# Converting the next batch block's edge-mask pieces on GpSimd at the head of each attention unit, instead of on VectorE between the row maxima

## The chip, the cores and the metric

The kernel runs on one core of a Trainium2 chip. The metric is the device time of one execution in microseconds (us), as the median of several runs. Engines are called PE (TensorE), DVE (VectorE), ACT (ScalarE), POOL (GpSimd) and SP (the sync engine, which here only issues DMAs).

## What is computed

A graph-attention layer over 2048 nodes of width 256 with a dense 2048 by 2048 edge mask, and after it a mixture of 8 experts, of which every token takes two. The part that matters here is the masked softmax of 8 heads:

```python
logits = jnp.einsum('thd,shd->hts', q, k)
logits = jnp.where(edge_mask[None] != 0, logits, NEG)
probs = jax.nn.softmax(logits, axis=-1)
ctx = jnp.einsum('hts,shd->thd', probs, v).reshape(T, D)
...
ht = layer_norm(ht, ln2_scale, ln2_bias)
ff = jax.nn.gelu(ht @ W1) @ W2
```

The expert layer behind it scatters rows to their two experts, runs two matrix products and a GELU per expert, and adds the weighted results back.

## The kernel before, in words

Four phases run one behind the other: layer norm and the projections (to about 88 us), attention (to about 707 us), the output projection with the feed-forward part and the routing, and the experts. The change lies in the attention, apart from one semaphore of the first phase.

Attention is cut into N = 32 units: 4 batch blocks of 512 target rows, and in each block 8 heads. Unit n is block b = n // 8 and head h = n % 8. Scores are made twice. The first time they have target rows in the partitions: PE makes 16 pieces of 128x512 per unit (`piece`, L826), and on each DVE adds the mask `maskA`, writes `masked` and takes the maximum of a row (`maxima`, L729); every fourth piece a short reduction closes a tile of 128 rows (L735), and ACT takes exponentials of it for the row sums (`row_sums`, L784). DVE and PE work here for unit n + 2 while unit n is finished. The second time (`key_scores`, L845) source rows lie in the partitions. The mask is added there by PE, which multiplies an identity with a piece of `maskB` into the same bank (L847); the shift by a row's maximum enters through extra rows of `qs` that SP copies there (`store_shift`, L527). ACT takes the exponentials (L807), and PE adds up the context (L859). PE runs its own written order of eight steps j in each unit; in step 3 stands a small transpose of the maxima for the next unit (`turn_negmax`, L833), once per unit.

`maskA` and `maskB` are bf16 tables of 0 and a large negative number, made from the int32 edge mask. `maskA` holds one block and is remade by four 128x2048 conversions on DVE, in head 5 of the block before (`mask_a`, L687, between the maxima behind pieces 3, 7, 11 and 15). `maskB` has two halves by `b % 2`, so that the next block's half is filled while this one's is read: in unit n, DVE converts one of the eight 128x1024 pieces of the next block between the maxima behind piece 7 (`mask_b`, L693, called from `beside` in `step`). That is 24 conversions in the units of blocks 0 to 2; block 3 has none. The eight conversions for block 0 come before unit 0. SP loads the int32 pieces into the two buffers of `adjB` (`load_adjB`, L520), each when the conversion before the last has freed its buffer, one unit ahead of use.

POOL spends this phase on work for later phases, one chain in each unit (L655 to L666): `scale_context` multiplies the context of unit n - 1 by the inverse row sums (L644, waits for DVE's L717 of that unit), `split` scales a 128x1024 piece of the expert weights and splits it in two f16 parts (L625, L629, L631), then come the DMA that stores them (L635), the load of the next piece (L620, into the single buffer `wch`) and two or three fills of expert rows (L638). What waits for L644 is SP, with the store of the context and the load of the next inverse sums, and through `context_out` the DVE addition L717 two units later.

The order of every engine is written by hand, and engines wait for each other by semaphores only. `maskB_ready` counts the conversions: PE waits for it in head 0 of a block, SP before it overwrites a buffer of `adjB`.

Of the kernel before, what the change touches and what calls it, by code (L numbers as in the profile page):

```python
# [5 lines left out]
ALU = mybir.AluOpType  # L6
# [9 lines left out]
P = 128  # L16
# [3 lines left out]
NO_EDGE = -(2.0**100)  # L20
# [10 lines left out]
def graph_attention_and_experts(nc, x, adj, adjT, nodemask, h_target, ln1_scale, ln1_bias, Wq, bq, Wk, bk, Wv, bv,  # L31
# [4 lines left out]
    H = 8  # L36
# [14 lines left out]
    with ctx:  # L51
        def sem(name):
            return ctx.enter_context(nc.semaphore(name))
# [57 lines left out]
        mask_in = sem("mask_in")  # L111
        bv_in = sem("bv_in")
        w_in = sem("w_in")
# [31 lines left out]
        with ph1:  # L145
# [24 lines left out]
            with block:  # L170
# [93 lines left out]
                def _(dve):  # L264
# [65 lines left out]
                    for g in range(NG):  # L330
                        tile_stats(1, hh, h_in, g)
                        if g % 2 == 1:
                            moments(1, g // 2, NT + GT * (g + 1))
                        if g + 1 < NG:
                            shift(xs, range(GT * (g + 1), GT * (g + 2)), xn_scaled, hs_ready)
                        if g == 1:
                            dve.wait_ge(w_in, 16 * 5)
                            split_low(0)
                            dve.wait_ge(bv_in, 16)
                            store_values(0)  # L340
# [9 lines left out]
                def _(act):  # L350
# [6 lines left out]
                    for n, w in enumerate((bk, bq)):  # L357
                        act.dma_start(bkq[:, n, :], w.rearrange("(c p) -> p c", p=P),
                                      allow_slow_non_contiguous=True).then_inc(w_in, 16)
                    act.dma_start(bv_b[:, :], bv.partition_broadcast(P)).then_inc(bv_in, 16)  # L360

# [22 lines left out]
                    normalise(0, xs, range(0, HT), xn_ready1)  # L384
                    act.wait_ge(w_in, 16 * 5)
                    act.activation(wqkv[:, 1, :, :], wqkv[:, 1, :, :], ACT.Copy, scale=QSCALE).then_inc(wq_scaled, 1)
# [12 lines left out]
                def _(pe):  # L399
# [34 lines left out]
                    turn(0)  # L434
                    pe.wait_ge(w_in, 16 * 5)
                    for k in range(2 * NG):
# [39 lines left out]
        maskA_ready = sem("maskA_ready")  # L476
        maskB_ready = sem("maskB_ready")
        adjB_in = [sem(f"adjB_in{i}") for i in range(2)]

        ph2 = ExitStack()  # L480
        with ph2:
# [26 lines left out]
            with block:  # L508
                @block.sync
                def _(sp):  # L510
# [55 lines left out]
                    for n in range(N):  # L566
# [6 lines left out]
                        if n + 1 + H < N:  # L573
                            sp.wait_ge(maskB_ready, H + n)
                            load_adjB(*divmod(n + 1 + H, H))
# [26 lines left out]
                def _(pool):  # L602
# [34 lines left out]
                    def prefill(row):  # L637
                        pool.dma_start(expert_rows[row, :].rearrange("(p a) d -> p (a d)", p=P),  # L638
                                       pad_rows.rearrange("(p a) d -> p (a d)", p=P)).then_inc(prefilled, 16)

                    def scale_context(n, h):
                        pool.wait_ge(context_summed, n + 2)
                        pool.wait_ge(inv_in, 32 * (n + 1))
                        pool.tensor_tensor(total[:, h % 2, :], total[:, h % 2, :], rT[:, :], ALU.mult)\  # L644
                            .then_inc(context_scaled, 1)
# [9 lines left out]
                    for n in range(N):  # L655
                        b, h = divmod(n, H)
                        e = 2 * b + h // 4
                        if n:
                            scale_context(n - 1, (n - 1) % H)
# [13 lines left out]
                def _(dve):  # L673
# [65 lines left out]
                    def step(n, b, h):  # L739
                        def beside(u):  # L740
                            if u == 5 and n:
                                add_halves(n - 1, *divmod(n - 1, H))
                            elif u == 7 and b + 1 < NB:

                                dve.wait_ge(scores_ready, 8 * H * b + 1)
                                mask_b(b + 1, h)
                            elif u == 4 and n + 1 < N:
# [70 lines left out]
                def _(pe):  # L818
# [17 lines left out]
                    def key_scores(n, b, h, j):  # L836

                        if j == 0:
                            pe.wait_ge(shift_rows[h % 4], 32 * (b * (H // 4) + h // 4 + 1))
                        if h == 0:  # L840
                            pe.wait_ge(maskB_ready, H * b + j + 1)
                        at_least(pe, weights_ready, 8 * n + j)
# [993 lines left out]
```

## Time and profile before

| | before |
|---|---|
| median of 3 runs | 1209.36 us (1206.07 to 1212.26) |
| profiled execution, own time | 1205.87 us |
| its span (first to last instruction) | 1203.6 us |
| mean granted TensorE clock | 0.926 of full speed |
| PE busy | 84% of the span |
| ACT busy | 64% |
| DVE busy | 60% |
| POOL busy | 42% |

The page is of one execution. Busy shares are over the whole span, across phases with different limits; the span is 2.3 us shorter than the same execution's own time, which has start and end around it. Times in the trace count from the first instruction. In rows of the timeline the number in square brackets is the idle time of that engine just before the instruction, with what ended it.

### The profile page before, as it was taken

To read this page: it belongs to the slowest core of one execution; us is meant where nothing else is said; L and a number is where in the kernel's file an instruction comes from. 1 tells how busy PE (TensorE), PEld (TensorE's weight loads), DVE (VectorE), ACT (ScalarE), POOL (GpSimd) and SP (SyncE) were. 2 spreads that over 40 slices of the span, in tenths; PEclk is the share of its full clock that TensorE was granted. 3 is DMA by queue.
4 is the path that set the end of the run, shared out by engine and by line. 5 is a ranking of instruction groups with operands and counts; after the bars stand their busy time and mean duration, and the time that the engine had idled before them with its cause. 6 is when DMAs were issued, how large, how long until landed. Compare 5 with 4: busy or idle time off the path is not lost. (4 is left out here: it accounts for less than half of the span.)

```text
span 1203.6 us, 22519 instructions
## 1 busy us (share of the span) xinstructions
PE 1008.1 (84%) x7088; PEld 620.1 (52%) x7089; DVE 721.9 (60%) x2011; ACT 770.8 (64%) x971; POOL 501.7 (42%) x453
## 2 busy tenths in 40 slices
PE   3934799899998999989999947798726999999994
PEld 2611344444444444434444415365614988888883
DVE  7816777888778878788777406545531443344332
ACT  4512589988988889989999822754113555545551
POOL 7405466456455465464466534000551322332232
PEclk9975699999999999999999978899957999999997
DMA  6596644753446433564433349510822323322333
GB/s 184 136 325 215 216 153 156 259 181 114 162 149 244 168 123 136 182 234 128 140 109 119 100 150 365 241 30 25 301 96 60 50 41 54 54 49 41 54 54 87
DMA packets 76178, 171.09 MB, mean 142 GB/s; under 512 B 13634, under 2 KB 45250, under 8 KB 70402
## 3 DMA queue, kind: packets, MB, share of 16 engines
q1 hardware_dynamic: 50962, 99.80, 24.9%
q0 software_dynamic: 21280, 69.11, 20.4%
q10 hardware_dynamic: 3856, 1.19, 0.5%
q8 instruction: 41, 0.67, 0.2%
q14 instruction: 39, 0.32, 0.1%
HBM read 123.05 MB, written 63.14 MB: 155 GB/s over the span
## 5 line engine op out<-in xcount | busy, mean ns | idle before, releaser
L729 DVE CUSTOM_DVE_ANT_0 masked<-ps,maskA 128x512 f32<-128x512 f32 x512 | 344.9, 687 | 111.3 <-PE ps L826 109.3
L826 PE MATMUL ps<-ks,qs 96*128 96x512 f32 x512 | 263.8, 550 | 71.5 <-DVE piecemax L729 46.8
L784 ACT ACTIVATE masked<-masked,negmax 128x2048 f32<-128x2048 f32 x128 | 256.3, 2003 | 67.9 <-DVE negmax L735 67.7
L807 ACT ACTIVATE weights<-ps 128x1024 f32<-128x1024 f32 x256 | 255.4, 1015 | 42.0 <-PE ps L847 40.6
L845 PE MATMUL ps<-qs,ks 98*128 98x512 f32 x512 | 230.3, 510 | 2.5 <-DMA qs<-shift_lo 1.7
L847 PE MATMUL ps<-maskB,identb 128*128 128x512 bf16 x512 | 202.8, 396 | 0.0
L826 PEld LDWEIGHTS ps<-ks,qs 96*128 96x128 f32 x512 | 102.7, 201 | 161.7 <-DVE piecemax L729 122.1
L1665 POOL DMA_INDIRECT sum_rows<-y,ids x48 | 74.3, 1548 | 206.0 <-issue 119.6
L1683 DVE TENSOR_TENSOR gT<-wall,gT 128x2048 f16<-128x2048 f32 x25 | 57.3, 2292 | 150.0 <-ACT gT L1733 150.0
L859 PE MATMUL ps<-weights,v_all 128*32 128x256 f32 x2048 | 137.0, 385 | 0.1
L1766 PE MATMUL ps<-xT,wall 128*128 128x256 f16 x1200 | 136.9, 275 | 0.0
L1779 PE MATMUL ps<-wall,gT 128*128 x1152 | 129.7, 273 | 0.0
L1766 PEld LDWEIGHTS ps<-xT,wall 128*128 x1200 | 118.3, 99 | 14.4 <-issue 0.3
L1779 PEld LDWEIGHTS ps<-wall,gT 128*128 128x128 f16 x1152 | 112.6, 98 | 13.2
L625 POOL TENSOR_SCALAR wch<-wch 128x1024 f32<-128x1024 f32 x36 | 100.5, 2792 | 42.7 <-DMA wch<-in_L_gnn_W 28.9
L1730 ACT ACTIVATE wall<-ps,b1s 128x256 f32<-128x256 f32 x200 | 83.4, 471 | 54.1 <-PE ps L1766 46.3
L847 PEld LDWEIGHTS ps<-maskB,identb 128*128 128x128 bf16 x512 | 50.4, 99 | 130.9 <-issue 129.0
L845 PEld LDWEIGHTS ps<-qs,ks 98*128 98x128 f32 x512 | 101.9, 199 | 18.0 <-ACT weights L807 8.7
L644 POOL TENSOR_TENSOR total<-total,rT 64x256 f32<-64x256 f32 x32 | 23.4, 732 | 204.9 <-DVE total L717 204.9
L859 PEld LDWEIGHTS ps<-weights,v_all 128*32 128x32 f32 x2048 | 53.4, 109 | 63.7 <-issue 40.9
L631 POOL TENSOR_TENSOR whl<-wch,whl 128x1024 f16<-128x1024 f32 x36 | 76.9, 2135 | 5.4 <-POOL whl L629 5.1
L1720 ACT ACTIVATE xT<-ps 128x512 f16<-128x512 f32 x26 | 15.5, 596 | 89.1 <-PE ps L1752 89.1
(178 smaller groups left out, 1174.7 us busy)
## 6 DMA issues: line engine op xcount, KB each, us to landing
expert_rows<-pad_rows POOLq DMA_DIRECT2D x73, 272.0 KB, 5.8
split_weights<-whl POOLq DMA_DIRECT2D x36, 512.0 KB, 3.4
wall<-split_weights SPq DMA_DIRECT2D x18, 1024.0 KB, 7.6
adjA<-in_adj SPq DMA_DIRECT2D x16, 1024.0 KB, 7.5
adjB<-in_adjT SPq DMA_DIRECT2D x32, 512.0 KB, 5.8
wch<-in_w1T POOLq DMA_DIRECT2D x16, 512.0 KB, 6.1
wch<-in_w2T POOLq DMA_DIRECT2D x16, 512.0 KB, 5.9
xr<-expert_rows SPq DMA_DIRECT2D x26, 272.0 KB
```

The lines of the kernel that those rows point to most:

```text
L625: pool.tensor_scalar(wch[:, :], wch[:, :], WSCALE, None, ALU.mult).then_inc(wch_scaled, 1)
L631: pool.tensor_tensor(whl[:, 1, :], wch[:, :], whl[:, 0, :], ALU.subtract).then_inc(wch_split, 1)
L729: dve.tensor_tensor_reduce(masked[:, a % 2, k * 512:(k + 1) * 512], ps[:, u % 2, :], maskA[:, a, k * 512:(k + 1) * 512], 1.0, NO_EDGE, ALU ...
L784: act.activation(masked[:, a % 2, :], masked[:, a % 2, :], ACT.Exp, bias=negmax[:, h % 2, a:a + 1], accum_out=rowsum[:, h % 4, a:a + 1]).t ...
L807: act.activation(weights[:, j % 4, :, :], ps[:, 2 + 2 * (j % 2):4 + 2 * (j % 2), :], ACT.Exp).then_inc(weights_ready, 1)
L826: pe.matmul(ps[:, u % 2, :], qs[0:KR, h % 4, a * P:(a + 1) * P], ks[0:KR, h, k * 512:(k + 1) * 512], start=True, stop=True)\
L845: pe.matmul(bank, ks[:, h, (2 * j + i) * P:(2 * j + i + 1) * P], qs[:, h % 4, :], start=True, stop=False)
L847: mm = pe.matmul(bank, identb[:, :], maskB[:, b % 2, 2 * j + i, :], start=False, stop=True)
L859: mm = pe.matmul(ps[at:at + HD, 6 + h % 2, 0:TB // 2], v_all[:, 2 * j + i, h * HD:(h + 1) * HD], weights[:, j % 4, i, t * (TB // 2):(t + 1 ...
L1730: act.activation(g4[:, m, :], ps[:, m // 2, m % 2 * PR:(m % 2 + 1) * PR], ACT.Gelu, bias=b1s[:, e, m:m + 1], scale=1.0 / WSCALE).then_inc( ...
L1766: mm = pe.matmul(ps[:, m // 2, m % 2 * PR:(m % 2 + 1) * PR], up(s, w, c, m), xT[:, q, x_, c, :], start=(n == 0 and c == 0), stop=(n == 2 a ...
L1779: mm = pe.matmul(ps[:, 4 + a, 0:D], gT4[:, g, q, m, a * P:(a + 1) * P], down(s, w, m), start=(m == 0 and n == 0), stop=(m == HC - 1 and n ...
```

## The change

The 24 conversions of later blocks' `maskB` pieces are issued by POOL as the first step of each unit, ahead of `scale_context`, with the same operation on the same tiles. They count on a semaphore of their own, `maskB_next`, for which SP and PE now wait; DVE keeps the eight conversions of block 0. In the first phase the load of `bv_b` counts on `w_in` with the other weights, so that the waits for `w_in` now want six loads instead of five, and `bv_in` is gone.

```diff
--- before.py
+++ after.py
@@ -109,7 +109,6 @@
         scale_in = sem("scale_in")
         shift_in = sem("shift_in")
         mask_in = sem("mask_in")
-        bv_in = sem("bv_in")
         w_in = sem("w_in")
         stat_step = sem("stat_step")
         stats_done = sem("stats_done")
@@ -334,9 +333,8 @@
                         if g + 1 < NG:
                             shift(xs, range(GT * (g + 1), GT * (g + 2)), xn_scaled, hs_ready)
                         if g == 1:
-                            dve.wait_ge(w_in, 16 * 5)
+                            dve.wait_ge(w_in, 16 * 6)
                             split_low(0)
-                            dve.wait_ge(bv_in, 16)
                             store_values(0)
                     for g in range(1, NG):
                         split_low(g)
@@ -357,7 +355,7 @@
                     for n, w in enumerate((bk, bq)):
                         act.dma_start(bkq[:, n, :], w.rearrange("(c p) -> p c", p=P),
                                       allow_slow_non_contiguous=True).then_inc(w_in, 16)
-                    act.dma_start(bv_b[:, :], bv.partition_broadcast(P)).then_inc(bv_in, 16)
+                    act.dma_start(bv_b[:, :], bv.partition_broadcast(P)).then_inc(w_in, 16)
 
                     def normalise(n, rows, tiles, done):
                         for i in tiles:
@@ -382,7 +380,7 @@
                                            ACT.Identity, bias=bkq[:, n, c:c + 1]).then_inc(kq_high, 1)
 
                     normalise(0, xs, range(0, HT), xn_ready1)
-                    act.wait_ge(w_in, 16 * 5)
+                    act.wait_ge(w_in, 16 * 6)
                     act.activation(wqkv[:, 1, :, :], wqkv[:, 1, :, :], ACT.Copy, scale=QSCALE).then_inc(wq_scaled, 1)
                     act.activation(bkq[:, 1, :], bkq[:, 1, :], ACT.Copy, scale=QSCALE).then_inc(wq_scaled, 1)
                     copy_turned(0)
@@ -432,7 +430,7 @@
                             mm.then_inc(v_ready, 1)
 
                     turn(0)
-                    pe.wait_ge(w_in, 16 * 5)
+                    pe.wait_ge(w_in, 16 * 6)
                     for k in range(2 * NG):
                         if k == NG:
                             pe.wait_ge(wq_scaled, 2)
@@ -475,6 +473,7 @@
         gap_zeroed = sem("gap_zeroed")
         maskA_ready = sem("maskA_ready")
         maskB_ready = sem("maskB_ready")
+        maskB_next = sem("maskB_next")
         adjB_in = [sem(f"adjB_in{i}") for i in range(2)]
 
         ph2 = ExitStack()
@@ -571,7 +570,10 @@
                             load_q(n + 3, (n + 3) // H, (n + 3) % H)
 
                         if n + 1 + H < N:
-                            sp.wait_ge(maskB_ready, H + n)
+                            if n:
+                                sp.wait_ge(maskB_next, n)
+                            else:
+                                sp.wait_ge(maskB_ready, H)
                             load_adjB(*divmod(n + 1 + H, H))
                         if n > 1:
                             store_context(n - 2, *divmod(n - 2, H))
@@ -638,6 +640,12 @@
                         pool.dma_start(expert_rows[row, :].rearrange("(p a) d -> p (a d)", p=P),
                                        pad_rows.rearrange("(p a) d -> p (a d)", p=P)).then_inc(prefilled, 16)
 
+                    def mask_b(b, h):
+                        pool.wait_ge(scores_ready, 8 * H * (b - 1) + 1)
+                        pool.wait_ge(adjB_in[h % 2], 16 * (b * (H // 2) + h // 2 + 1))
+                        pool.tensor_scalar(maskB[:, b % 2, 2 * h:2 * h + 2, :], adjB[:, h % 2, :, :], 0.0, NO_EDGE,
+                                           ALU.is_equal, ALU.mult).then_inc(maskB_next, 1)
+
                     def scale_context(n, h):
                         pool.wait_ge(context_summed, n + 2)
                         pool.wait_ge(inv_in, 32 * (n + 1))
@@ -655,6 +663,8 @@
                     for n in range(N):
                         b, h = divmod(n, H)
                         e = 2 * b + h // 4
+                        if b + 1 < NB:
+                            mask_b(b + 1, h)
                         if n:
                             scale_context(n - 1, (n - 1) % H)
                         split(n + 4)
@@ -740,10 +750,6 @@
                         def beside(u):
                             if u == 5 and n:
                                 add_halves(n - 1, *divmod(n - 1, H))
-                            elif u == 7 and b + 1 < NB:
-
-                                dve.wait_ge(scores_ready, 8 * H * b + 1)
-                                mask_b(b + 1, h)
                             elif u == 4 and n + 1 < N:
                                 invert_sums(n + 1, (n + 1) % 4, (n + 1) % 2)
                             elif u == 9 and n + 1 < N:
@@ -837,8 +843,10 @@
 
                         if j == 0:
                             pe.wait_ge(shift_rows[h % 4], 32 * (b * (H // 4) + h // 4 + 1))
-                        if h == 0:
-                            pe.wait_ge(maskB_ready, H * b + j + 1)
+                        if h == 0 and b == 0:
+                            pe.wait_ge(maskB_ready, j + 1)
+                        elif h == 0:
+                            pe.wait_ge(maskB_next, H * (b - 1) + j + 1)
                         at_least(pe, weights_ready, 8 * n + j)
                         for i in range(2):
                             bank = ps[:, 2 + 2 * (j % 2) + i, :]
```

On POOL, in a unit of block 0 before:

```order
L638 DMA expert_rows<-pad_rows 16x4352 x2
L644 TENSOR_TENSOR total<-total,rT 64x256
L625 TENSOR_SCALAR wch<-wch 128x1024
L629 CAST whl<-wch 128x1024
L631 TENSOR_TENSOR whl<-wch,whl 128x1024
L635 DMA split_weights<-whl 256x1x1024
L620 DMA wch<-in_w2T 128x4x256
```

and the same place now:

```order
L640 DMA expert_rows<-pad_rows 16x4352 x2
L646 TENSOR_SCALAR maskB<-adjB 128x1024
L652 TENSOR_TENSOR total<-total,rT 64x256
L627 TENSOR_SCALAR wch<-wch 128x1024
L631 CAST whl<-wch 128x1024
L633 TENSOR_TENSOR whl<-wch,whl 128x1024
L637 DMA split_weights<-whl 256x1x1024
```

The conversion has moved in between the last fill of one unit and the scaling of the context.

On DVE, behind piece 7 of the maxima in head 5 of a block, where both masks were converted, before:

```order
L729 ISA piecemax 128x1
L735 TENSOR_REDUCE negmax<-piecemax 128x4
L693 TENSOR_SCALAR maskB<-adjB 128x1024
L687 TENSOR_SCALAR maskA<-adjA 128x2048
L729 ISA masked,piecemax<-ps,maskA 128x512
```

and now:

```order
L739 ISA piecemax 128x1
L745 TENSOR_REDUCE negmax<-piecemax 128x4
L697 TENSOR_SCALAR maskA<-adjA 128x2048
L739 ISA masked,piecemax<-ps,maskA 128x512
```

L693 is gone from here and from the same place of the other units of blocks 0 to 2; nothing else of DVE has moved.

## Rows read from the trace of the kernel before

**Rows 1.** Busy time by engine in two stretches of the attention (blocks 0 to 2, and 3).

```profile
256.70:383.30 126.60, 117.72 (x792) 53.87 (x791) 100.48 (x295) 113.59 (x121) 66.08 (x58) 1.00 0.48 160
...
586.00:685.40 99.40, 98.59 (x673) 45.74 (x673) 71.82 (x233) 95.19 (x101) 56.66 (x50) 1.00 0.37 117
```

**Rows 2.** Waits in the stretch 256.7 to 383.3: us in total, times, longest.

```profile
PE ps L826 <- DVE piecemax L729: 8.9, 15, 1.0
```

**Rows 3.** Timeline, the transpose L833, one per unit: start, duration.

```profile
147.50 0.27 PE L833 MATMUL ps<-ident,negmax 128*36 128x128 f32 x1
164.39 0.27 PE L833 MATMUL ps<-ident,negmax 128*36 128x128 f32 x1
...
236.25 0.27 PE L833 MATMUL ps<-ident,negmax 128*36 128x128 f32 x1
256.71 0.27 PE L833 MATMUL ps<-ident,negmax 128*36 128x128 f32 x1
...
440.21 0.27 PE L833 MATMUL ps<-ident,negmax 128*36 128x128 f32 x1
...
512.20 0.27 PE L833 MATMUL ps<-ident,negmax 128*36 128x128 f32 x1
...
586.40 0.27 PE L833 MATMUL ps<-ident,negmax 128*36 128x128 f32 x1
...
669.46 0.27 PE L833 MATMUL ps<-ident,negmax 128*36 128x128 f32 x1
```

**Rows 4.** The conversions L693: summary (min/median/max ns) and one on the timeline.

```profile
L693 DVE TENSOR_SCALAR maskB<-adjB x32: 682/1755/1909, 119.4 to 569.5; 128x1024 bf16<-128x1024 int32 x32
```

```profile
165.51 0.70 DVE L693 TENSOR_SCALAR maskB<-adjB 128x1024 bf16<-128x1024 int32 x1
```

**Rows 5.** Timeline around a conversion of a regular unit.

```profile
310.45 2.77 POOL L625 TENSOR_SCALAR wch<-wch 128x1024 f32<-128x1024 f32 x1
...
311.94 1.83 DVE L693 TENSOR_SCALAR maskB<-adjB 128x1024 bf16<-128x1024 int32 x1
...
314.42 0.50 PE L826 MATMUL ps<-ks,qs 96*128 96x512 f32 x1 [0.70 <-DVE piecemax L729]
```

**Rows 6.** Timeline of POOL: a unit's first and last step, and a first step of block 3.

```profile
255.69 0.73 POOL L644 TENSOR_TENSOR total<-total,rT 64x256 f32<-64x256 f32 x1 [8.42 <-DVE total L717]
...
264.94 1.13 POOL L638 DMA_DIRECT2D expert_rows<-pad_rows  x2
```

```profile
618.52 0.72 POOL L644 TENSOR_TENSOR total<-total,rT 64x256 f32<-64x256 f32 x1 [6.55 <-DVE total L717]
```

**Rows 7.** POOL's groups by line: busy, mean ns, idle before.

```profile
L625 POOL TENSOR_SCALAR wch<-wch 128x1024 f32<-128x1024 f32 x36 | 100.5, 2792 | 42.7 <-DMA wch<-in_L_gnn_W 28.9 <-DMA wch<-in_w1T 7.7 <-DMA wch<-in_w2T 6.1
```

**Rows 8.** Timeline of head 5 in block 0: conversions on DVE, and POOL's last step.

```profile
237.38 0.70 DVE L693 TENSOR_SCALAR maskB<-adjB 128x1024 bf16<-128x1024 int32 x1
238.00 2.35 DVE L687 TENSOR_SCALAR maskA<-adjA 128x2048 bf16<-128x2048 int32 x1
...
246.21 1.05 POOL L638 DMA_DIRECT2D expert_rows<-pad_rows  x2
...
249.18 1.22 DVE L687 TENSOR_SCALAR maskA<-adjA 128x2048 bf16<-128x2048 int32 x1
```

**Rows 9.** Summary of the maxima L729 (min/median/max ns).

```profile
L729 DVE CUSTOM_DVE_ANT_0 masked<-ps,maskA x512: 658/692/695, 97.0 to 678.3; 128x512 f32<-128x512 f32 x171
```

**Rows 10.** Loads of adjB: one issue, and the page's row (KB, us to landing).

```profile
303.90 0.42 SPq L520 DMA_DIRECT2D adjB<-in_adjT  x1
```

```profile
adjB<-in_adjT SPq DMA_DIRECT2D x32, 512.0 KB, 5.8
```

**Rows 11.** Timeline of PE in the second unit: a wait for the shift rows.

```profile
173.83 0.51 PE L845 MATMUL ps<-qs,ks 98*128 98x512 f32 x1 [1.71 <-DMA qs<-shift_lo]
```

**Rows 12.** Timeline of ACT in the first phase.

```profile
16.96 0.63 ACT L386 ACTIVATE wqkv<-wqkv 128x512 f32<-128x512 f32 x1 [1.18 <-DMA bkq<-in_L_gnn_bq]
...
18.57 1.02 ACT L372 ACTIVATE sT<-ps 128x1024 f32<-128x1024 f32 x1 [0.88 <-PE ps L410]
```

## Prediction

> **What bounds the kernel now.** I read first the busy time of each engine inside the attention, in a stretch of seven units from the end of block 0 through block 1 and in block 3, because only block 3 runs without conversions of masks [rows 1]. In both the granted clock is full. In the first PE is busy 117.7 of 126.6 us, in the second 98.6 of 99.4 us: the last block is bound by PE alone, the others lose time on it. The waits say on what: PE stands for DVE's maxima, 15 times and 8.9 us in the first stretch, up to 1.0 us at once [rows 2], as if something long stood in DVE's way. Then I took a clock that the program has itself, the transpose L833, of which each unit has one. Its starts give the length of a unit [rows 3]. Four regular units from 440.21 to 512.20 take 71.99 us, 18.00 each. The first five intervals of block 3 take 83.06 us, 16.61 each. The first interval of all takes 16.89, and the one with head 5's conversions of maskA 20.46. So a regular unit pays 1.39 us for something that block 3 doesn't have.
>
> That something is L693. Its own summary is uneven: 682 ns at best, 1755 at the median [rows 4]. The timeline tells why. The conversion at 311.94 lasts 1.83 us and ends at 313.77, while POOL's L625 runs from 310.45 to 313.22; that end and some 0.55 us make the end of DVE's. PE's next piece stands 0.70 us after it [rows 5]. The one at 165.51, with L625 not running, lasts 0.70 [rows 4]. So two thirds of what DVE pays is a wait for POOL, with DVE's whole queue of maxima behind it, and PE behind those.
>
> **The change, part by part.**
>
> 1. Regular units. 24 intervals lie between the first transpose and the one at 586.40. Three are head 5 (below). The first three have a short conversion of 0.7 us, the fourth one of a length between; for these I take 16.89 - 16.61 = 0.28 us each three times, and 0.9 once, midway between 0.28 and 1.39: 1.7 us. The other 17 fall from 18.00 to 16.61: 17 x 1.39 = 23.6 us. That is what PE loses, and not the 1.8 us that DVE does, because what DVE is late by is in part made up by its slack.
>
> 2. Head 5, three times. DVE has four conversions of maskA there beside L693 and is the bound of a unit of 20.46 us. L693 takes 0.62 us from start to start there (237.38 to 238.00) [rows 8], so 3 x 0.6 = 1.9 us are saved.
>
> 3. POOL gets 24 conversions of 128x1024, and no row shows such an operation on it. The nearest is L625, the same shape and kind with one arithmetic step instead of two and f32 on both sides: 2.79 us [rows 7]. Below I go to half of it, 1.4 us, since the output is half as wide; above to 5.6 us, a full pass for either step. I take 2.8. It is hidden: POOL's steps run from 255.69 to 266.07, 10.4 us [rows 6], and then it stands for 8.4 us until DVE's L717 lets the next unit's L644 go, in block 3 still for 6.55 us [rows 6]. The conversion falls exactly into that gap, ahead of L644. If the cover is gone, that is over 6.5 us, L644 is late, and behind it the split, SP's store of the context and its loads of the inverse sums, which stand in the queue ahead of the next unit's loads.
>
> 4. Its inputs. SP issues a piece (303.90) a unit ahead and it lands in 5.8 us [rows 10], while POOL's unit, in which it is wanted, reaches it some 16 us later. SP's wait before the load asks for the conversion two pieces earlier, which POOL finishes earlier in the unit than DVE did. Nothing is past its time: 0. In head 0 of a block PE wants the first piece, converted seven units before, and the last, converted at the start of the unit before: 0.
>
> 5. What collides anew. POOL's last fill in head 5 ends at 246.21 + 1.05 = 247.26, so the new conversion runs from there to 250.1. DVE's fourth conversion of maskA started at 249.18 and now would start 0.6 us earlier, at 248.6 [rows 8]. By what rows 5 show it then stands until POOL is done and needs its own 1.22 us: about 251.3 in place of 249.8, 1.5 us, in a unit that DVE bounds. Three times that is 4.5 us lost. The second conversion of maskA (2.35 us at 238.00) starts 0.6 us earlier in POOL's L625. The 0.70 us one that started at that place ran freely; if maskA's does too, each head 5 saves 1.1 us more. I count 0 and keep 3.3 us for the lower end.
>
> 6. The semaphore of the first phase. ACT's L386 now waits also for bv_b, the next load on its queue. Before, it stood 1.18 us for bq and its next step stood 0.88 us for PE [rows 12], so up to 0.9 us of lateness costs nothing there. I take 0, and 1 us for the upper end.
>
> Sum: 23.6 + 1.7 + 1.9 - 4.5 = 22.7 us. Against the profiled execution's own 1205.87 us this gives 1183.2; the median of the runs is 3.5 us above that execution, so I forecast 1209.36 - 22.7 = **1186.7 us**.
>
> What the trace shows of the pair of engines is that DVE's conversion and POOL's instructions shut each other out, 0.70 us against 1.83 [rows 4, 5]. The Trainium skill (Perfetto Trace Analysis, Optimizing Scalar/DVE Operations) speaks against this change: DVE and GpSimd share an SBUF port, so moving work between the two "might not help". By that rule, carried over to every DVE instruction, the time would be that of the third rival below. The trace agrees with it for the conversions and not for the maxima.
>
> **The rivals.**
>
> *A smaller gain.* The conversion on POOL takes 4 to 5.6 us. It still fits into 6.55 us. But POOL's early units, where the weight loads keep it behind, slip against DVE. One unit there already shows what comes of it, 1.71 us of PE's waiting for shift rows whose copy was issued just behind POOL's transfers [rows 11]; two more such waits are 3.4 us. And each collision in head 5 grows by the 2.8 us that the conversion is longer, 8.4 us in all. 22.7 - 3.4 - 8.4 = 10.9 us, 1198.5 us. For it: two arithmetic steps with a comparison and an integer input, of which no row has either. Against: L625 is already slow for one step, as if it had room for two.
>
> *POOL becomes the bound, slower than before.* With 10.4 us of other steps, POOL sets the unit once the conversion is over 16.61 - 10.4 = 6.2 us, and decides against the change once it is over 18.0 - 10.4 = 7.6 us. At 9 us, a unit is 19.4 us: 24 x 19.4 = 466 against the 438.9 us that those intervals take now [rows 3], and head 5 as before with its 20.5: about 27 us more, 1236 us. For it: POOL's price is in no row. Against: it would need over three times L625's.
>
> *The maxima stand for POOL too.* If they used what POOL shares with DVE, the new instruction would hold DVE 2.8 us in each unit, in place of 1.83: 1 us more per unit, some 21 us in all, 1230 us. Against: 512 maxima lie between 658 and 695 ns [rows 9] though POOL works half of that time; none is longer.
>
> *It does nothing.* DVE was late by its conversion, but PE is then held by ACT instead, which is busy 113.6 of 126.6 us [rows 1]. Then the time stays within 5 us of before, 1207. Against: in block 3 the same ACT work fits in 16.61 us.
>
> **How the numbers follow.** A measurement of this kernel can tell about 0.5%, 6 us, from no change. The forecast has a chance of 0.74, with a range of its own of 1180 (no collision paid in head 5, and more from L687) to 1193 us (maskA's collisions doubled, 1 us lost in the first phase). A smaller gain has 0.13, POOL as the bound 0.08, the maxima's stand 0.02, and nothing 0.03. Faster by over 0.5% are the first two, 0.87; within 0.5% is the last, 0.03, with 0.01 of the slower cases, where POOL takes about 7.6 us; slower is 0.09. The range that leaves out the last three and most of the ends goes from 1178 to 1199 us: its lower end is 22.7 + 3.3 + 4.5 = 30.5 us below the median, its upper end the smaller gain.
>
> **What would show it.** In the changed kernel's trace, regular transposes of blocks 0 to 2 are 16.6 us apart, and those of head 5 near 21. L693's place on DVE is empty, and PE's longest wait for a maximum in a regular unit is as in block 3. POOL's new group of 24 has a mean of 2.8 us, and the idle time before the context's scaling falls from some 8.4 to 3.8 us (6.55 - 2.8) and is not zero. The fourth conversion of maskA in head 5 is 2.7 us and no longer 1.22. The forecast is wrong if the unit stays over 17 us with DVE not converting, if POOL's idle time goes to zero, or if the conversion takes over 4 us.

## The result, and the profile after

The changed kernel takes 1177.72 us (median of 4 runs, 1173.21 to 1178.63) against 1208.72 us of the kernel before on the same occasion: a ratio of 0.9734 (95% interval 0.9698 to 0.9771), 31.0 us less. The forecast was 22.7 us less. The direction and the place were right; the time lies 9.0 us below the forecast and 0.3 us below the lower end of its range.

The transposes of the changed kernel (L839, L833 before), for [rows 3]:

```profile
147.67 0.27 PE L839 MATMUL ps<-ident,negmax 128*36 128x128 f32 x1
...
233.13 0.27 PE L839 MATMUL ps<-ident,negmax 128*36 128x128 f32 x1
251.71 0.27 PE L839 MATMUL ps<-ident,negmax 128*36 128x128 f32 x1
...
420.16 0.27 PE L839 MATMUL ps<-ident,negmax 128*36 128x128 f32 x1
...
486.44 0.27 PE L839 MATMUL ps<-ident,negmax 128*36 128x128 f32 x1
...
555.19 0.27 PE L839 MATMUL ps<-ident,negmax 128*36 128x128 f32 x1
```

The 24 intervals from first to last take 407.52 us in place of 438.90: 31.4 us, nearly the whole 32.2 us by which the span is shorter. Four regular units from 420.16 take 16.57 us each, before 18.00. Adding up the intervals of the whole list, the 17 regular ones give 23.6 us (18.11 us each before, 16.72 now), the first four 2.7 us, the three of head 5 5.1 us (the first of them is 18.58 us, before 20.46).

Busy time in a regular stretch, for [rows 1] (us of the stretch, then PE, PE's weight loads, DVE, ACT and POOL busy with counts, granted clock, DMA share, GB/s), and PE's waits from 256.7 to 383.3, for [rows 2]:

```profile
251.70:368.30 116.60, 116.23 (x779) 54.38 (x791) 89.79 (x288) 112.77 (x121) 89.93 (x65) 1.00 0.52 174
```

```profile
PE ps L832 <- DVE piecemax L739: 2.2, 5, 0.6
```

PE is now busy in all but 0.4 us of this stretch, as it was in block 3 alone; its wait for maxima is 2.2 us in place of 8.9. That window already runs into head 5 of block 1 here; over the same seven units, 251.7 to 368.3, the wait is 0.4 us, once. POOL has gone from half to three quarters of the stretch and is still no bound.

The new group on POOL, by its summary (min/median/max ns), and POOL's wait ahead of the context's scaling:

```profile
L646 POOL TENSOR_SCALAR maskB<-adjB x24: 3652/3656/4713, 153.6 to 531.2; 128x1024 bf16<-128x1024 int32 x24
```

```profile
300.28 0.73 POOL L652 TENSOR_TENSOR total<-total,rT 64x256 f32<-64x256 f32 x1 [3.01 <-DVE total L727]
```

The conversion takes 3.66 us there, where DVE needs 0.69 alone. The longest, 4.71 us, is one beside which DVE started a conversion of maskA (experiment 1). The gap of 8.4 us ahead of the scaling [rows 6] has become one of some 3 us.

Head 5 of block 0, for [rows 8], on the timeline:

```profile
233.35 3.00 POOL L627 TENSOR_SCALAR wch<-wch 128x1024 f32<-128x1024 f32 x1
234.24 1.23 DVE L697 TENSOR_SCALAR maskA<-adjA 128x2048 bf16<-128x2048 int32 x1
...
237.67 2.15 POOL L633 TENSOR_TENSOR whl<-wch,whl 128x1024 f16<-128x1024 f32 x1 [0.15 <-POOL whl L631]
238.96 1.95 DVE L697 TENSOR_SCALAR maskA<-adjA 128x2048 bf16<-128x2048 int32 x1
...
243.09 3.66 POOL L646 TENSOR_SCALAR maskB<-adjB 128x1024 bf16<-128x1024 int32 x1
244.19 1.22 DVE L697 TENSOR_SCALAR maskA<-adjA 128x2048 bf16<-128x2048 int32 x1
```

Here the forecast fails. The fourth conversion of maskA starts 1.10 us into POOL's new one, as forecast, and doesn't wait: 1.22 us, and POOL's is as long as all others. The second starts 0.89 us into the multiplication and is free too, where it took 2.35 us before [rows 8], 1.1 us more than alone; this time POOL paid, 3.00 in place of 2.77 us. Only the third is late, by 0.73 us, behind a subtraction.

### The profile page after: what moved, and what is told of

Same layout as the page of the kernel before. It is cut to its first block and busy times, and to the rows that moved or that the text cites. A ratio compares the mean times of both kernels' runs of the same rounds, so it can differ in the third digit from the quotient of the medians.

```text
span 1171.4 us, 22454 instructions
## 1 busy us (share of the span) xinstructions
PE 1000.4 (85%) x7024; PEld 618.9 (53%) x7089; DVE 690.7 (59%) x1987; ACT 768.5 (66%) x971; POOL 583.0 (50%) x477
## 5 line engine op out<-in xcount | busy, mean ns | idle before, releaser
L832 PE MATMUL ps<-ks,qs 96*128 96x512 f32 x512 | 259.4, 546 | 46.7 <-DMA qs<-q_low 24.3
L813 ACT ACTIVATE weights<-ps 128x1024 f32<-128x1024 f32 x256 | 253.1, 1015 | 18.1 <-PE ps L855 14.6
L855 PE MATMUL ps<-maskB,identb 128*128 128x512 bf16 x448 | 175.9, 393 | 0.0
L646 POOL TENSOR_SCALAR maskB<-adjB 128x1024 bf16<-128x1024 int32 x24 | 88.8, 3698 | 1.9
```

The costliest lines, as they stand in the source:

```text
L646: pool.tensor_scalar(maskB[:, b % 2, 2 * h:2 * h + 2, :], adjB[:, h % 2, :, :], 0.0, NO_EDGE, ALU.is_equal, ALU.mult).then_inc(maskB_next, 1)
L813: act.activation(weights[:, j % 4, :, :], ps[:, 2 + 2 * (j % 2):4 + 2 * (j % 2), :], ACT.Exp).then_inc(weights_ready, 1)
L832: pe.matmul(ps[:, u % 2, :], qs[0:KR, h % 4, a * P:(a + 1) * P], ks[0:KR, h, k * 512:(k + 1) * 512], start=True, stop=True)\
L855: mm = pe.matmul(bank, identb[:, :], maskB[:, b % 2, 2 * j + i, :], start=False, stop=True)
```

## What is to be told apart

Theory A is the forecast's: an instruction of POOL holds what it shares with DVE from start to end. The rows above speak against it, so theory B: a `tensor_scalar` of POOL (the multiplication, the mask conversion) holds it in parts only. Two more questions decide what the change is worth: whether DVE's work or its wait was the cost, so whether POOL was needed at all, and whether POOL's 3.66 us cost anything.

## The experiments

**1. The pair by itself.** 38 trials in a kernel of their own. POOL starts one instruction when DVE gives the signal, DVE starts a conversion after a fill of growing length. The core of it:

```diff
+ ins = pool.tensor_scalar(pf[:, :], pf[:, :], 1.0, None, ALU.mult)
+ ins = pool.tensor_scalar(pm[:, :, :], pi[:, :, :], 0.0, NO_EDGE, ALU.is_equal, ALU.mult)
+ ins = pool.tensor_tensor(ph[:, :], pf[:, :], pg[:, :], ALU.subtract)
+ ins = pool.tensor_copy(ph[:, :], pf[:, :])
...
+ dve.memset(fill[:, 1:1 + part], 0.0).then_inc(b_fill, 1)
+ dve.wait_ge(b_fill, f)
+ dve.tensor_scalar(bm[:, :, :], bi[:, :, :], 0.0, NO_EDGE, ALU.is_equal, ALU.mult)
```

> This kernel leaves out the whole computation: it copies x to the output and then runs 38 trials. In each, POOL starts one instruction on 128x1024 (a multiplication f32 to f32 in place as the weight split's first step; the mask conversion int32 to bf16 with two steps; a subtraction of two f32 tiles to f16; a cast f32 to f16), and DVE starts the 128x1024 mask conversion (0.69 us when alone) after a fill of 0 to 3.6 us. Theory A, the pair is held from a POOL instruction's start to its end (the forecast's): every DVE conversion that starts inside a POOL instruction ends 0.55 us after POOL's end, and POOL keeps its length (2.77, 3.66, 2.13, 1.04 us). Theory B, POOL holds it only for a part: for POOL's mask conversion and its multiplication there is a stretch of starts, around 0.9 to 1.2 us behind POOL's, where DVE takes 0.69 us and POOL is not or hardly longer; starts at 1.4 us and later behind the multiplication wait for its end.

The timeline, for the multiplication (L94) with DVE's conversion (L120) at three offsets:

```profile
16.13 2.77 POOL L94 TENSOR_SCALAR bench_pf<-bench_pf 128x1024 f32<-128x1024 f32 x1 [0.21 <-DVE bench_fill L112]
...
16.46 1.25 DVE L120 TENSOR_SCALAR bench_mask<-bench_int 128x1024 bf16<-128x1024 int32 x1
...
25.05 2.77 POOL L94 TENSOR_SCALAR bench_pf<-bench_pf 128x1024 f32<-128x1024 f32 x1 [0.21 <-DVE bench_fill L112]
...
26.17 0.69 DVE L120 TENSOR_SCALAR bench_mask<-bench_int 128x1024 bf16<-128x1024 int32 x1
...
31.32 2.77 POOL L94 TENSOR_SCALAR bench_pf<-bench_pf 128x1024 f32<-128x1024 f32 x1 [0.21 <-DVE bench_fill L112]
...
33.09 1.55 DVE L120 TENSOR_SCALAR bench_mask<-bench_int 128x1024 bf16<-128x1024 int32 x1
```

and for the mask conversion on POOL (L96):

```profile
65.85 3.63 POOL L96 TENSOR_SCALAR bench_pmask<-bench_pint 128x1024 bf16<-128x1024 int32 x1 [0.21 <-DVE bench_fill L112]
...
66.86 0.69 DVE L120 TENSOR_SCALAR bench_mask<-bench_int 128x1024 bf16<-128x1024 int32 x1
...
81.22 4.10 POOL L96 TENSOR_SCALAR bench_pmask<-bench_pint 128x1024 bf16<-128x1024 int32 x1 [0.21 <-DVE bench_fill L112]
...
83.74 0.70 DVE L120 TENSOR_SCALAR bench_mask<-bench_int 128x1024 bf16<-128x1024 int32 x1
```

Read each pair by offset (DVE's start less POOL's) and by DVE's end. Behind the multiplication, starts at 0.33, 0.60 and 0.85 us all end 1.57 to 1.59 us after POOL's start: DVE waits until about 1.03 and then needs 0.55. Starts at 1.12 us are free. At 1.51 us DVE is free and POOL takes 3.09 us. Starts at 1.77 and 2.02 us end 0.55 us behind POOL's end. So POOL holds what it shares with DVE twice, in its first 1.03 us and about its last one, with a gap between. (The holds are inferred from when DVE gets through; the trace doesn't show them.) Behind POOL's mask conversion the gap is wider: starts at 1.01, 1.46 and 1.77 us are free, and with the one at 2.52 us POOL pays 0.47 us. The subtraction and the cast show no gap: started 0.39 us into a subtraction of 2.34 us, DVE takes 2.49, and every start up to 2.08 us into it, or 0.72 us into the cast, ends 0.55 us behind POOL's end.

Theory B holds, A falls. It also reads [rows 5] and [rows 8] of before: in regular units L693 started 1.49 us into L625 and met its second hold, in head 5 at 0.89 us, where it went through, and L687 behind it met the hold in its place. POOL's instruction beside [rows 8]:

```profile
236.49 2.76 POOL L625 TENSOR_SCALAR wch<-wch 128x1024 f32<-128x1024 f32 x1
```

One thing doesn't fit to a tenth. In the trials a start at 1.51 us into the multiplication still goes through and one at 1.77 waits, while in the regular units of the kernel starts from 1.41 to 1.58 us wait; yet a conversion of maskA ahead of unit 0, 1.53 us into L625, goes through and POOL takes 3.64 us. For POOL's mask conversion the kernels and the trials agree: a start at 2.61 us goes through (POOL 4.71 us, changed kernel), one at 2.65 waits (experiment 9, halves). Where the second hold begins for L693 in a regular unit stays open.

**2. DVE's conversion seven pieces later, without POOL.** On the kernel before:

```diff
-                            elif u == 7 and b + 1 < NB:
+                            elif u == 14 and b + 1 < NB:
```

> The kernel before with DVE's conversion of maskB behind piece 14 of the maxima instead of behind piece 7, where POOL stands idle. Theory A and B alike (what DVE pays is a wait for POOL's instruction, 1.83 against 0.70 us): the 20 conversions that were long fall to 0.70 us, regular units from 18.0 to 16.9 us, the time to about 1188 us, so two thirds of the change's gain without POOL. Rival (what counts is that DVE has the work at all): units stay near 18.0 us, 1206 to 1209 us.

1175.80 us, 0.9735 of before (0.9696 to 0.9773). The whole gain, from one number. The summary of L693 (min/median/max ns) and PE's wait for maxima in the stretch 256.7 to 383.3:

```profile
L693 DVE TENSOR_SCALAR maskB<-adjB x32: 683/690/1790, 118.8 to 549.5; 128x1024 bf16<-128x1024 int32 x32
```

```profile
PE ps L826 <- DVE piecemax L729: 1.7, 4, 0.6
```

The median conversion is 690 ns, before 1755 [rows 4]. Over the same seven units as in [rows 2] PE's wait is 0.3 us, once. The 17 regular intervals take 284.2 us, to a tenth as in the changed kernel. What was expected too high, 16.9 us a unit, was the cost of a short conversion: behind piece 14 it is hidden in DVE's slack and costs under 0.1 us, for the regular unit is 16.72 us here and in the changed kernel. Head 5's three units are as with the change too, 18.6 us each.

**3. No conversion at all in the later blocks.** On the changed kernel; blocks 1 to 3 read a constant half of maskB and so attend to nothing:

```diff
+                    pool.memset(maskB[:, 1, :, :], NO_EDGE).then_inc(maskB_next, 1)
...
-                        if b + 1 < NB:
-                            mask_b(b + 1, h)
...
-                            mm = pe.matmul(bank, identb[:, :], maskB[:, b % 2, 2 * j + i, :], start=False, stop=True)
+                            mm = pe.matmul(bank, identb[:, :], maskB[:, min(b, 1), 2 * j + i, :], start=False, stop=True)
```

> The changed kernel without the 24 conversions of later blocks: every piece of blocks 1 to 3 reads a half of maskB that is filled once with the large negative number, so these blocks attend to nothing. If POOL's conversions are wholly hidden: regular units 16.6 us, head 5 units 18.5 us, 1176 to 1179 us as the changed kernel. If they still cost something in head 5, where maskA is converted beside them (the forecast's 1.5 us each): head 5 units 0.5 to 1.5 us shorter than the changed kernel's 18.56, 1173 to 1175 us.

1176.74 us, 0.9745 (0.9714 to 0.9776): the changed kernel's time. This kernel has something of its own ahead of unit 0: POOL's fill of half of maskB takes 6.95 us, and DVE's first conversion of maskA, started 0.63 us into it, takes 7.41 us. So the intervals say more than the time. Head 5's units are 18.56 us each, against 18.58, 18.54 and 18.56, and all 24 intervals take 406.3 us against 407.5 and, when the changed kernel ran again (experiment 9), 406.9. POOL's 24 conversions cost nothing that can be told from the scatter, in head 5 neither.

**4. POOL's load doubled.** On the changed kernel, each conversion issued twice:

```diff
+                        for i in range(2):
+                            at_least(pool, maskB_next, done + i)
                             pool.tensor_scalar(maskB[:, b % 2, 2 * h:2 * h + 2, :], adjB[:, h % 2, :, :], 0.0, NO_EDGE,
```

> The changed kernel with each of the 24 conversions issued twice on POOL, the second to the same place. POOL's steps then take 10.13 + 2 x 3.66 + 0.2 = 17.6 us a unit against 16.61 for PE. If POOL's sum alone sets the unit: regular units 17.6 us, no idle time before the context's scaling, 24 x 1.0 less what head 5 hides, about 1177.7 + 18 = 1196 us. If its lateness is hidden for some units by the slack that the queues have: under 1190 us. If late inverse sums and loads add waits of their own: units over 18.2 us, above 1208 us, slower than before.

1201.97 us, 0.9942 (0.9920 to 0.9964), some 24 us over the changed kernel. The 24 intervals take 437.75 us, 18.24 each, where POOL's own sum is 17.6: neither the first expectation nor the third. And the units aren't even. Several are 16.6 us, then one is 17.4 to 27.3. The timeline of the first such unit shows what POOL's lateness does:

```profile
216.54 1.52 SPq L547 DMA_DIRECT2D rT<-inv_rows  x2
...
219.50 0.42 SPq L519 DMA_DIRECT2D adjB<-in_adjT  x1
...
220.95 0.90 SPq L516 DMA_DIRECT2D adjA<-in_adj  x2
...
222.51 0.58 SPq L526 DMA_DIRECT2D qs<-shift_lo  x1
...
230.82 0.79 PE L856 MATMUL ps<-qs,ks 98*128 98x512 f32 x1 [6.87 <-DMA qs<-shift_lo]
```

SP stood in its queue for the context's scaling, 11.6 us, before it loaded the inverse sums. So the loads behind it, 0.5 MB of adjB and 2 MB of adjA, were issued right ahead of the shift rows, and PE waited 6.87 us for a row of 2 KB. From 222.5 to 230.8 the DMA engines' busy share was 1.00; POOL's own transfers, issued from 223.24 on, ran there too, and no run separates the two. The second unit's 1.71 us [rows 11] are a wait for shift rows as well, but not behind such loads: SP had issued none since 157.5, while POOL had issued its store, its load and two fills from 166.24 to 168.5, and the DMA engines were busy for 99% of 168 to 172.

**5. One piece earlier.** On the kernel before, `u == 6` for `u == 7`, where DVE meets POOL's first hold.

> The kernel before with DVE's conversion of maskB behind piece 6 instead of 7, where it meets the first pass of POOL's multiplication (about 0.3 us behind its start) and not the second. Theory B (POOL holds the pair for about 1.03 us at either end of its two-step instructions): the conversion takes 1.2 to 1.35 us, ends 1.55 to 1.6 us behind POOL's start, and the regular unit lies between the 16.7 us that a 0.70 us conversion gives and the 18.1 us of a 1.83 us one: about 17.4 us, the time about 1188 us. Theory A (held from start to end): 3 us long conversions, units over 19 us. Rival (the place alone counts, not the wait): 18.1 us, no change.

1185.39 us, 0.9828 (0.9807 to 0.9850). A typical pair on the timeline:

```profile
301.71 2.77 POOL L625 TENSOR_SCALAR wch<-wch 128x1024 f32<-128x1024 f32 x1
301.87 1.42 DVE L693 TENSOR_SCALAR maskB<-adjB 128x1024 bf16<-128x1024 int32 x1
```

It ends 1.58 us behind POOL's start, as in the trials. The regular unit is 17.25 us on average. With 0.69 us giving 16.7, 1.42 giving 17.25 and 1.83 giving 18.1, the unit grows with the wait, and the more the longer it is. The place counts too, but for less: in the third interval of the kernel before, the conversion behind piece 7 took 0.70 us, delayed by nobody, and the interval was 16.88 us, against 16.62 in the changed kernel and 16.48 with the conversion behind piece 14. That is some 0.3 us of the 1.39; the rest goes with the wait.

**6. Head 5 in the other order.** On the kernel before, maskA's conversion ahead of maskB's behind piece 7:

```diff
-                            elif u == 7 and b + 1 < NB:
+                            elif u == 7 and b + 1 < NB and h != H - 3:
...
                                 mask_a(b + 1, u // UPT)
+                                if u == 7:
+                                    dve.wait_ge(scores_ready, 8 * H * b + 1)
+                                    mask_b(b + 1, h)
```

> The kernel before with the two conversions behind piece 7 of head 5 in the other order, maskA's first. Theory B: maskA's, which starts some 0.9 us behind POOL's multiplication, takes 1.22 to 1.3 us in place of 2.35, POOL's multiplication about 3.0 in place of 2.76; maskB's behind it meets the second pass and takes 1.3 to 1.5 us in place of 0.70; head 5 units are 0.2 to 0.5 us shorter. Theory A: maskA's waits for POOL's end as before, 2.9 to 3.0 us, since it starts 0.6 us earlier. The time as a whole within the noise of before, 1204 to 1210 us.

```profile
238.35 3.00 POOL L625 TENSOR_SCALAR wch<-wch 128x1024 f32<-128x1024 f32 x1
239.23 1.24 DVE L687 TENSOR_SCALAR maskA<-adjA 128x2048 bf16<-128x2048 int32 x1
240.39 1.51 DVE L693 TENSOR_SCALAR maskB<-adjB 128x1024 bf16<-128x1024 int32 x1
```

One run of 1205.17 us, as expected. The durations are those of theory B. The length of head 5's units wasn't as expected, 21.94, 19.32 and 20.19 us, and led to the clock. Windows of the kernel before in head 5 of blocks 0, 1 and 2 (columns as above), and PE's wait ahead of them in block 0:

```profile
240.00:244.00 4.00, 3.00 (x8) 1.64 (x8) 3.12 (x11) 1.14 (x2) 3.36 (x2) 0.66 0.63 223
387.00:391.00 4.00, 2.93 (x7) 1.71 (x8) 3.08 (x10) 0.90 (x2) 3.43 (x2) 0.63 0.65 211
534.00:538.00 4.00, 2.16 (x8) 1.01 (x8) 3.90 (x12) 1.84 (x2) 3.69 (x2) 1.00 0.56 197
```

```profile
241.00 0.56 PE L826 MATMUL ps<-ks,qs 96*128 96x512 f32 x1 [1.97 <-DVE piecemax L729]
```

Behind the two conversions PE stood for 2.0 us, in each of the three blocks. In blocks 0 and 1 the granted clock then had a mean of 0.66 and 0.63 over 4 us (part of them at the lower of its two levels, 1.2 of 2.4 GHz), and the units took 20.46 and 20.70 us; in block 2 it stayed at full, and the unit took 19.64. Experiment 6 has the same split: PE stood for 1.7 us in each block, the granted clock over the 4 us behind was 0.62, 1.00 and 0.57, and the one unit at full clock, 19.32 us, is 0.3 us shorter than the 19.64 of before, as theory B had it. With the change all three stay at 1.00 and at 18.6 us.

**7. The other part of the change alone**, bv_b's load counted on `w_in`, on the kernel before:

```diff
-                            dve.wait_ge(w_in, 16 * 5)
+                            dve.wait_ge(w_in, 16 * 6)
                             split_low(0)
-                            dve.wait_ge(bv_in, 16)
...
-                    act.dma_start(bv_b[:, :], bv.partition_broadcast(P)).then_inc(bv_in, 16)
+                    act.dma_start(bv_b[:, :], bv.partition_broadcast(P)).then_inc(w_in, 16)
```

> The kernel before with only the change's other part: the load of bv_b counts on w_in and all waits for w_in want six loads. If it costs nothing: L386 starts up to 1 us later, the first copy of turned rows at the same 18.6 us, the first transpose L833 within 0.3 us of 147.5, the time that of before, 1205 to 1211 us. If it lies on the path: 1 us more at the first L833 and in the end.

1203.81 us, 0.9990 (0.9971 to 1.0010). ACT's wait ends 0.2 us later, at 17.15, and its next copy stands for PE as before [rows 12]:

```profile
17.15 0.63 ACT L384 ACTIVATE wqkv<-wqkv 128x512 f32<-128x512 f32 x1 [1.38 <-DMA bv_b<-in_L_gnn_bv]
...
18.36 1.02 ACT L370 ACTIVATE sT<-ps 128x1024 f32<-128x1024 f32 x1 [0.48 <-PE ps L408]
```

The attention of this kernel is that of the kernel before, so its trace is a second look at head 5. PE stands there for 2.0 us again in each block, the granted clock over the 4 us behind has a mean of 0.62, 0.79 and 0.66, and the units take 22.19, 21.23 and 22.35 us: 65.8 us for the three against 60.8. How much head 5 loses to the clock differs from one execution to the next.

**8. MaskA in halves, outside POOL's holds.** What is left over block 3's pace is head 5 (18.6 us) and the unit before it (17.1 us). On the changed kernel:

```diff
+        HALVES = {(5, 3): (0, 0), (5, 7): (0, 1), (5, 12): (1, 0), (5, 14): (1, 1),
+                  (6, 3): (2, 0), (6, 4): (2, 1), (6, 7): (3, 0), (6, 11): (3, 1)}
...
-                                mask_a(b + 1, u // UPT)
+                            if b + 1 < NB and (h, u) in HALVES:
+                                mask_half(b + 1, *HALVES[h, u])
```

> The changed kernel with maskA's four 128x2048 conversions of head 5 cut in eight of 128x1024 and spread over heads 5 and 6, each behind a piece where POOL doesn't hold the pair (pieces 3, 7, 12, 14 of head 5; 3, 4, 7, 11 of head 6), and with the loads of adjA moved to match. If DVE's slack in a unit hides a 0.7 us conversion as it did behind piece 14 (0.05 us each): head 5 units fall from 18.56 to about 17.1 us, those next to them stay at 16.6 to 17.0, 4 to 6 us in all, about 1172 us. If it is the sum of DVE's work in head 5 that counts: two conversions fewer there, 17.5 us, but head 6 pays as much as is saved, 1176 to 1178 us as the changed kernel.

1172.67 us, 0.9722 (0.9703 to 0.9741). Head 5's units fall to 17.0 us, but the next ones rise from 16.4 to 17.9, and there two of the eight halves land on a hold after all, one on the first hold of POOL's multiplication (1.03 us) and one on a subtraction (1.68 us).

```profile
250.49 1.03 DVE L717 TENSOR_SCALAR maskA<-adjA 128x1024 bf16<-128x1024 int32 x1
255.04 1.68 DVE L717 TENSOR_SCALAR maskA<-adjA 128x1024 bf16<-128x1024 int32 x1
```

**9. The three side by side**, five rounds on one chip, each with its expectation:

> The changed kernel once more, beside the two others of this group on one chip: 0.973 to 0.976 of before. It is here to tell the others apart from it.

> DVE's conversion behind piece 14 once more. The traces give it 411.5 us between the first transpose and the 25th against 407.5 of the changed kernel, all of the difference in the first four units: 2 to 4 us longer than the changed kernel, 0.976 to 0.978 of before. If the position alone were worth the whole change in every part: the same within 1 us.

> MaskA in halves over heads 5 and 6 once more. Its trace gives 405.6 us for the same 24 intervals against 407.5: 2 us shorter than the changed kernel (0.17%), 0.971 to 0.973 of before. If that is only the scatter of one execution: no difference, intervals that overlap in full.

| kernel | median us | ratio to before | interval |
|---|---|---|---|
| changed | 1173.49 | 0.9725 | 0.9689 to 0.9762 |
| DVE behind piece 14 | 1174.34 | 0.9734 | 0.9699 to 0.9770 |
| changed, maskA in halves | 1170.11 | 0.9697 | 0.9662 to 0.9731 |

Before was 1206.04 us here. The conversion on POOL and the one on DVE behind piece 14 can't be told apart: 0.85 us, where 2 to 4 were expected. The traces have 3.4 us between them again, 2.5 of them in the first four units, where PE waits for shift rows. The halves' median lies 3.4 us below the changed kernel's here, but the intervals overlap, and the traces don't bear out so much: head 5 with its two neighbours is 1.6 us shorter over the three blocks in the first pair of traces and 0.4 us in the second. That gain is not shown.

## Why the prediction was right or wrong

1. *Regular units, 23.6 us.* Measured 23.6 us over the 17 intervals. That about block 3's pace is what is left when DVE doesn't stand was right. The exact number is in part luck: 18.00 and 16.61 us both lie 0.1 us below the 17 units' means, 18.11 and 16.72, and the difference stays.
2. *The first four, 1.7 us.* Measured 2.7. The wait for the shift rows in the second unit was 1.13 us this time and not 1.71. (Midway between 0.28 and 1.39 is 0.84 and not 0.9, which changes nothing.)
3. *Head 5, a saving of 1.9 us less 4.5 us of new collisions.* This is the step that failed. Forecast was a loss of 2.6 us over three units, measured a gain of 5.1, and this 7.7 us is most of the 9.0 by which the forecast missed (the rest is the first units and the scatter of the runs). Three things were wrong in it. The collision with the new conversion, 3 x 1.5 us, doesn't exist (experiments 1 and 3): POOL doesn't hold what it shares with DVE in the middle of it, and the fourth conversion of maskA took 1.22 us and not 2.7. The second conversion of maskA became free, 3 x 1.1 us, which the text had in its lower end and counted as 0, though [rows 8] had L693 free at the same offset. And the two units in which the clock had dipped got back some 0.8 and 1.1 us, of which nothing was forecast. Against these stands the third conversion, late by 0.7 us three times; together 7.5 of the 7.7 us. The clock's part belongs to the two executions compared: against head 5 as experiment 7's trace has it the gain would be 10.1 us and not 5.1.
4. *POOL's price, 2.8 us between 1.4 and 5.6.* Measured 3.66. That it is hidden was right, with 3 us to spare where 3.8 was forecast.
5. *Inputs and the first phase, 0.* Right (experiment 7 for the latter).
6. *The lower end, 1178 us.* Its sum, 30.5 us below the median, is 1178.9 us. It took the free L687 and the absent collisions in; the third conversion's lateness, the clock and the first units weren't in it. That the time lies 0.3 us below 1178 means little by itself, where the four runs lie 5.4 us apart.

Of the rivals, POOL as the bound was rightly unlikely; its mechanism is real and costs more than its sum (experiment 4). Its example was added up wrong: 21 units of 19.4 us and three of 20.5 take 469 us, 30 us more than before and not 27. The smaller gain rested on longer collisions, which aren't there. The maxima don't wait for POOL: with POOL busy in 77% of the stretch all 512 still lie between 658 and 693 ns. The Trainium skill (Perfetto Trace Analysis, Optimizing Scalar/DVE Operations) says that, because the two share a port, offloading between them might not help. The traces agree that DVE and POOL shut each other out (1.83 us against 0.70), but here the move helped, by 31.0 us. What helped is that the conversion no longer starts in one of POOL's holds, and one number in DVE's order does the same as the move to POOL.

## What to carry to other kernels

When one instruction's duration has two values, find what the other engine does at its start before moving it elsewhere: here a shift by seven pieces on the same engine gave all of 31 us. Price a stall by the offset into the other engine's instruction, not by whether the two overlap. Where the stall stands ahead of a PE-bound order, look also at the granted clock behind it.

## What the runs showed of the hardware that was not expected

- GpSimd's `tensor_scalar` on 128x1024 (2.77 us for a multiplication, 3.66 us for a mask conversion) shuts VectorE's conversions out only in its first 1.03 us and its last 1 us or so. Between, VectorE's 0.69 us instruction runs at full speed and GpSimd's isn't longer. A subtraction of two tiles (2.34 us) and a cast (1.04 us) hold at every offset tried, and so does a fill of 6.95 us at the one offset seen.
- The exclusion works both ways: a conversion that starts shortly before the second hold runs at once, and GpSimd's instruction grows (to 3.00, 3.09 and 4.10 us, and to 4.71 us beside a conversion of 128x2048).
- Behind 2.0 us of waiting in head 5, PE's granted clock fell in five of six otherwise equal places (0.66 and 0.63 in two of three in the kernel before, 0.62, 0.79 and 0.66 in all three of experiment 7's trace, each over 4 us), and the units took 0.8 to 2.7 us more than the one at full clock. What decides between them stays open.
